# A two-engine pipeline over sixteen images, with five images written out in each lap of the loop

## The reference

```python
h = layernorm(x) * (1 + ca) + sa
x = x + ga * mamba(h)          # conv, selective scan over 256 steps with 256 x 16 states, gate
h = layernorm(x) * (1 + cb) + sb
x = x + gb * moe(h)            # 8 experts of width 64, two of them chosen, and a shared one
h = layernorm(x) * (1 + ca1) + sa1
x = x + ga1 * gated_delta(h)   # 8 heads, short convolutions, delta rule in chunks of 128 tokens
h = layernorm(x) * (1 + cb1) + sb1
x = x + gb1 * attend_experts(h)  # softmax attention, then 8 dense experts of width 512
```

## Time and profile before

| what | value |
|---|---|
| median of 3 runs | 2821.86 us (2817.24 to 2822.73) |
| span of the profiled execution, first to last instruction | 2813.2 us |
| what the profiled execution took around its span | not listed on its own; the median is 8.7 us above the span |
| mean granted clock of PE | 0.938 of full speed |
| instruction transfers, whole span | 208 of 16 KB, 97 of 8 KB |

### The profile page before, as it was taken

One profiled execution on the slowest core, in us unless ns is written; L12 is line 12 of the kernel. 1 busy time (PEld: TensorE's weight loads), 2 busy tenths in 40 slices (PEclk: granted clock), 3 DMA queues, 4 the chain that ended last, 5 costly groups with the idle time before them and its releaser, 6 DMA issues.

```text
span 2813.2 us, 61085 instructions
## 1 busy us (share of the span) xinstructions
PE 2441.0 (87%) x22584; PEld 1893.0 (67%) x22584; DVE 2212.7 (79%) x5136; ACT 1200.1 (43%) x2697; POOL 549.1 (20%) x497
## 2 busy tenths in 40 slices
PE   3688989888898988989888898988989889898997
PEld 2466768667686766768667586766758667686776
DVE  6677897878879887787878879887887978879742
ACT  3332536344353543436444353543536444253512
POOL 2122221122222022121112222022121112222010
PEclk7789999999999999999999999999999999999998
DMA  4000000000000000000000000000000000000000
GB/s 132 4 2 3 7 4 1 8 3 8 3 7 2 3 8 3 7 3 4 5 3 8 3 7 2 3 8 3 7 3 5 4 3 8 3 7 2 1 6 3
DMA packets 24835, 21.46 MB, mean 8 GB/s; under 512 B 7218, under 2 KB 21571, under 8 KB 24531
## 3 DMA queue, kind: packets, MB, share of 16 engines
q1 hardware_dynamic: 24530, 17.26, 2.2%
HBM read 15.13 MB, written 2.13 MB: 6 GB/s over the span
## 4 chain that ended last, share of the span: by engine, by line
PE 32%; issue 32%; DVE 27%; POOL 4%; ACT 2%; DVEq 0%; POOLq 0%; ACTq 0%
DVE wide L1382 4%; DVE wide L1394 3%; PE banks L891 3%; PE banks L1198 3%; PE banks L1024 3%; PE banks L1188 3%; DVE wide L1402 3%; PE banks L1016 2%; PE banks L1052 2%; DVE inv L1570 2%; PE banks L1005 2%; DVE inv L1566 2%; PE banks L963 1%; PE banks L1065 1%; DVE inv L1557 1%
## 5 line engine op out<-in xcount | busy, mean ns | idle before, releaser
L1519 DVE SCALAR_TENSOR_TENSOR wide<-pad,conv,wide 128x256 f32<-128x256 f32 x864 | 370.0, 496 | 0.0
L561 POOL TENSOR_TENSOR wide<-wide 128x512 f32<-128x512 f32 x128 | 188.3, 1471 | 832.0 <-DVE wide L1402 472.0
L1394 DVE TENSOR_TENSOR_SCAN wide<-wide 128x1024 f32<-128x1024 f32 x128 | 292.9, 2288 | 1.9 <-ACT wide L667 0.3
L667 ACT ACTIVATE wide<-small,a_neg 128x255 f32<-128x255 f32 x512 | 216.0, 496 | 173.9 <-DVE wide L1394 173.0
L1044 PE MATMUL banks<-hideb,identb 128*128 128x512 bf16 x800 | 272.1, 403 | 0.0
L1188 PE MATMUL banks<-inv,up 128*128 128x256 f32 x1024 | 264.5, 387 | 0.0
L1198 PE MATMUL banks<-down,inv 128*128 128x128 f32 x2048 | 256.5, 276 | 0.0
L1198 PEld LDWEIGHTS banks<-down,inv 128*128 128x128 f32 x2048 | 248.7, 192 | 5.0
L796 ACT ACTIVATE inv<-banks,up1b 128x256 f32<-128x256 f32 x512 | 214.0, 480 | 52.0 <-PE banks L1188 51.5
L1024 PEld LDWEIGHTS banks<-inv,mats 64*64 64x64 f32 x5120 | 168.3, 139 | 63.9 <-issue 62.1
L1024 PEld LDWEIGHTS banks<-inv 64*64 64x64 f32 x5120 | 159.5, 135 | 67.4 <-issue 65.3
(11 more groups left out here) (280 smaller groups left out, 4933.4 us busy)
## 6 DMA issues: line engine op xcount, KB each, us to landing
gates_bc<-gate_rows SPq DMA_DIRECT2D x32, 128.0 KB, 2.9
x<-in_x SPq DMA_DIRECT2D x16, 128.0 KB, 2.1
up<-in_W SPq DMA_DIRECT2D x1, 2048.0 KB
out<-xn_y SPq DMA_DIRECT2D x16, 128.0 KB, 2.1
wide<-in_wmod SPq DMA_DIRECT2D x2, 384.0 KB, 5.6
con<-in_con SPq DMA_DIRECT2D x1, 724.0 KB, 4.7
w_k<-in_Wk SPq DMA_DIRECT2D x1, 512.0 KB
w_q<-in_Wq SPq DMA_DIRECT2D x1, 512.0 KB
```

What stands on the lines that cost most here:

```text
L561: g.tensor_tensor(ypart[p % 2], r[:, 0:512], r[:, 512:1024], ALU.add).then_inc(a_yp.h, 1)
L667: last = s.activation(decay[st % 2][:, at + 1:at + T], dt[:, c, 1:T], ACT.Exp, scale=a_neg[:, c, st * SG + q:st * SG + q + 1])
L1394: v.tensor_tensor_scan(state[st % 2], decay[st % 2], drive[st % 2], 0.0, ALU.mult, ALU.add).then_inc(a_h.h, 1)
L1519: v.scalar_tensor_tensor(dst, src, w, dst, ALU.mult, ALU.add).then_inc(c_conv.h, 1)
```

## The change

The loop of `follow` runs over laps of PER_TURN = 5 images. In a lap the same interleaved list of steps is written out five times, with i = 5 * lap + 1 to 5 * lap + 5 for the first half and one less for the second. 15 laps become 3. The order of the steps, the waits and their values are the same; the straight code ahead of the loop and behind it stays, and so does SP's loop.

```diff
+PER_TURN = 5
...
-            with eng.Fori(1, NB) as i:
-                at = {"x": 0, "y": 0}
-                for half in turns:
-                    name, *args = (first if half == "x" else second)[at[half]]
-                    at[half] += 1
-                    steps[name](i if half == "x" else i - 1, *args)
+            assert (NB - 1) % PER_TURN == 0
+            with eng.Fori(0, (NB - 1) // PER_TURN) as lap:
+                for n in range(PER_TURN):
+                    i = lap * PER_TURN + (n + 1)
+                    at = {"x": 0, "y": 0}
+                    for half in turns:
+                        name, *args = (first if half == "x" else second)[at[half]]
+                        at[half] += 1
+                        steps[name](i if half == "x" else lap * PER_TURN + n, *args)
```

## The result

| | before | changed |
|---|---|---|
| median of 4 runs | 2821.77 us (2817.24 to 2822.73) | 2771.64 us (2770.77 to 2773.63) |
| ratio, 95% interval | | 0.9826 (0.9802 to 0.9850) |
| span of the profiled execution | 2813.2 us | 2769.0 us |
| what the profiled execution took | not listed | 2770.77 us |
| mean granted clock of PE | 0.938 | 0.942 |

Faster by 50 us between the medians and by 44 us between the two traces. 38 were forecast. These four runs of the kernel before are on the slow side of it: in the 55 that were taken later beside the experiments, in three groups, its median was 2812.4, 2815.0 and 2816.7 us, and against those the changed kernel is 41 to 45 us faster.

The account below looks back on a forecast made before the run. Bound by PE and DVE handing work to each other in strict order, both stalling at jumps back. Twelve jumps removed at 3.2 us give 38 us: 2821.9 - 38.4 = 2783.5 us, range 2768 to 2805.

Parts of the forecast that it names:

- The price of a jump: At each removed jump back: PE's idle 1.90 us plus slower work up to L1547, 3.17 us, taken as 3.2.
- The second way, by whole laps: Price of a jump from comparing jumping laps with the one that falls through: 3.64 us, 44 us for 12.
- PE's side sets it: At the jump PE's delay, not DVE's 2.65 us stall, decides when L1547 starts; 3.2 us taken.
- more than the sum: Rival: 44 us or a little more saved, 2776 down to 2768 us; chance counted with the forecast's 0.72.
- 8.7 us around the span: Median of the runs lies 8.7 us above the profiled span, for what surrounds the first and last instruction.
- Added register work: Register arithmetic for the waits in each image: taken as nothing, 8 us kept in the range.
- ACT and POOL at the two remaining jumps: With longer bodies they may have to fetch at the jumps that stay: 0 to 5 us, taken as 0.
- ACT's fetches in straight code: ACT's body no longer stays resident: about 3.7 blocks per image, 55 over 15 images, taken as costing nothing.
- POOL's gmask: PE's input tile behind the edge, needed at 492.70 and there at 491.74: 0.96 us of room.
- Idle time alone: Rival: only PE's idle time at the jumps is gained, 12 x 1.9 = 23 us, 2799 us; chance 0.19.
- The edge isn't the jump: Rival: the gap where the loop turns back has another cause and stays, 2822 us; chance 0.04.
- Slower, ACT streams: Rival: half of ACT's 55 block fetches become visible inside the handovers, 73 us lost, 2857 us; chance 0.05.

Follow-up runs that it names:

- e3: Kernel before with five images per lap on PE and DVE only, ACT and POOL keeping 15 laps; 2773.3 us, ratio 0.9870.
- e4: Kernel before, still 15 laps, with a hint naming the jump's target ahead; 2801.35 us, ratio 0.9963.
- e9: Kernel before, 15 laps, with the jump hint and PE's loop head placed on the start of a 16 KB block; 2770.65 us, ratio 0.9852.
- e7: Changed kernel, laps of five images, with the jump hint added at the head of each lap; 2764.51 us, ratio 0.9827 against the kernel before.
- e1: Kernel before with five images per lap on PE only, DVE, ACT and POOL keeping 15 laps; 2802.3 us, ratio 0.9965.
- e8: Kernel before with no loop on PE, DVE, ACT and POOL, all 16 images written out; 2757.75 us, ratio 0.9791.
- e2: Kernel before with five images per lap on DVE only, PE, ACT and POOL keeping 15 laps; 2812.1 us, ratio 0.9998.

## Why the prediction was right, and which term was small

**Where the time is.** Shown: the gain is that of the 12 jumps, on PE and DVE together (e3), and of the fetch behind them, not of the branch or of the lap's length (e4, e9).

**The price of a jump.** The term was 3.17 us, 3.2 in the sum: PE's idle time and the slower stretch up to the first L1547. Between the same two instructions the runs show 5.53 - 2.15 = 3.38. Of the 0.21 between them 0.14 had been left out (at a seam L1005 overlaps the end of L997); 0.04 is a slip in the mean from L1005 to L1547, which is 3.63 and not 3.59 over the 14 edges; 0.03 is the seam being shorter than the fall-through.

The second way, by whole laps, had given 3.64, and e7 seems to bear it out: 168.17 - 164.54 = 3.63 us per image. But e9, which takes all 14 jumps, is 168.17 - 165.06 = 3.1 us per image faster, and its edges are 5.53 - 2.43 = 3.1 us shorter. What is left of an image, from L1547 to the end of the next L997, is 162.8 us before, 162.6 in e9, 162.5 in the changed kernel and 162.4 in e7, and from lap to lap it goes from 162.0 to 164.1 in the kernel before. So the last quarter of a microsecond is not shown to be the jump's. The 3.64 rested on one lap, in which that remainder was 162.51 against 162.78 on the mean of the 13 before it: 0.27 of the 3.64 is this.

**Which side sets it.** "PE's side sets it" holds at the ten edges where the clock fell. At the other four L1547 starts 4.56 to 4.87 us after L997, 1.2 us after the start of DVE's statistics, just as at the 12 edges of e1 where PE does not stall at all (4.57 to 4.91). So some 0.8 of the 3.4 us (5.53 less 4.70, the mean of the four) goes with the falls of the clock; without a fall DVE's own stall holds L1547 there. e1's 10 us are about 0.8 us for each of the 12 jumps.

**The sum against the runs.** 12 x 3.38 = 41 us of the 44 by which the traces differ; the other 3 lie in the rest of the images, 0.2 for each, and no run says what they are. The median fell by 50, to 2771.6, 11 us below the likeliest time and inside the band 2768 to 2776 that the prediction called "more than the sum" and gave to a price of 3.64 and fewer falls of the clock. That it got there is in part the sample. "8.7 us around the span" was a mistaken step: the changed kernel's profiled execution took 2770.77 us for a span of 2769.0, 1.8 around it. So the profiled execution of before took about 2815 us, below all four runs behind the median of 2821.77 but in the middle of the 55 later ones. Those scatter from 2801 to 2830 us, e9 from 2770 to 2776 over 5. Such a scatter is what one expects where falls of the clock may or may not meet an edge; that is argued, not shown.

**The parts that were costed at nothing.** Added register work: 61085 to 60548 instructions, 537 fewer, so it was not added but saved a little. ACT and POOL at the two remaining jumps: nothing (e3). ACT's fetches in straight code: e3 and the changed kernel differ only in the loops of ACT and POOL, and have 72 and 118 transfers of 8 KB, so these two engines fetch 46 blocks more. 55 had been worked out for ACT; the window of the earlier trace rows holds the six transfers of DVE's lap and the first of the next, not seven of one. ACT has no wait put down to issue, and the time is the same. POOL's gmask: not the next wait, at the seams PE starts L1009 without a gap. x and gate rows: no new wait for a DMA.

**The rivals.** "Idle time alone" (2799) is refuted by the seams, where L1551 comes at 2.15 us and the clock stays at 1.00. "The edge isn't the jump" is refuted: the rows put down to issue went from 14 to 2 with the jumps. With the target named ahead all jumps are taken and DVE's gap comes down to 0.4 us, PE's to nothing (e4, e9). The Trainium skill's 108 ns for a compare-and-branch (Advanced Engine Details and Errata, Control Flow Timing) are not the whole price of these jumps: the trace has 1.90 and 2.65 us. "Slower, ACT streams" is refuted by e3 and e8.

What stays open: what the last 7 us between e7 and e8 consist of, the 3 us outside the edges, the single stall that comes with the hint, and why the granted clock falls behind some stalls and not behind others of the same length.

## What to carry to other kernels

In a kernel of hand-ordered engine streams, look among the waits put down to issue for a count that equals the number of jumps back; if the instructions named are the first of a loop body, suspect the fetch of the loop's head. Here it cost 2 to 3 us on each engine whose body did not stay resident. Write several laps out, or write it straight, or name the jump's target ahead and see to it that the jump does not stand at the beginning of its block; treat the engines together, since freeing one alone gave 0 or 10 us of 39. For the price, compare the same two instructions at an edge that jumps and at one that does not, for instance where the last lap falls through; a single whole lap carries the scatter of everything else in it.

## What the runs showed of the hardware

- At a jump back in a loop of one image PE idles 1.90 us and DVE 2.65 on the mean of 14. A 16 KB transfer of PE begins 0.9 to 1.1 us behind its jump at all 14, an 8 KB one of DVE 1.0 to 1.3 us behind its own. ACT starts its next work when its input is there.
- The hint alone took DVE's stall from 2.65 to 0.4 us and PE's from 1.9 to between 0.7 and 2.1 (1.2 on the mean). With PE's jump some 118 instructions into its block in place of the first few, PE's went to nothing. The place without the hint left PE's idle time at 1.86 us, at 2807.95 us.
- The hint brought DVE one stall of 1.5 to 2.1 us in the straight code behind the loop (e4, e7, e9).
- Instructions come in 16 KB for PE (208 transfers before, 186 with its laps of five, e1) and in 8 KB for DVE (97 and 72, e2) and for ACT and POOL (72 in e3, 118 in the changed kernel). In e8, all straight code, no matmul of PE has a wait put down to issue, and DVE has one of 1.4 us and one of 0.2.
- With the hint, the waits view names POOL as the releaser of PE's idle time at 9 edges. That POOL was not the cause is shown by e9, where the same POOL work is in the same place and PE does not wait.
